# Block copies by DMA and 32x32 transposes on VectorE in place of TensorE transposes, in a two-layer cross-attention kernel

## What is computed

```
q = x Wq + bq;  k = ctx Wk + bk;  v = ctx Wv + bv
w = softmax(q k^T / sqrt(512)) over the 224 rows of x (axis 1), not over the 750 of the context
x = layernorm(w v + x) * gamma + beta
```

## Time and profile before

| what | value |
|---|---|
| three runs | 1115.15, 1117.38 (median), 1117.8 us |
| profiled execution | span 1115.5 us from its first to its last instruction; what lies around the span is not listed |
| span against the median | 1.9 us shorter |
| busy share of the span: PE, PEld, DVE, ACT, POOL | 94, 88, 79, 71, 70% |
| DMA queues | 60 MB, 16.8% of 16 engines |

### The profile page before, as it was taken

How to read it: one execution, slowest core, us unless ns; L and a number is a source line. 1 busy time by engine, 2 the same in 40 slices (tenths; PEclk the granted TensorE clock), 3 DMA queues, 4 the chain that set the end, 5 groups by cost and what they waited for, 6 DMA issues and landing times.

```text
span 1115.5 us, 26568 instructions
## 1 busy us (share of the span) xinstructions
PE 1050.1 (94%) x8392; PEld 981.2 (88%) x8392; DVE 879.5 (79%) x2561; ACT 788.8 (71%) x2033; POOL 775.8 (70%) x646
## 2 busy tenths in 40 slices
PE   4999999999999999999999999999999999999973
PEld 3888999899989999999999989998998999899973
DVE  1557888888888888888888888888888888888864
ACT  1446777777777777777777777777777777777733
POOL 0034787777777877777787777777877777778754
PEclk8898999999999999999999999999999999999987
DMA  8121101111110111111101111111011111111001
GB/s 214 40 87 40 37 32 62 62 62 60 60 44 33 44 60 60 60 60 56 41 26 58 60 60 60 60 51 39 31 60 60 60 60 60 44 35 43 18 17 33
DMA packets 19218, 60.15 MB, mean 54 GB/s; under 512 B 4064, under 2 KB 6112, under 8 KB 19184
## 3 DMA queue, kind: packets, MB, share of 16 engines
q1 hardware_dynamic: 16544, 59.71, 16.4%
q10 hardware_dynamic: 2640, 0.01, 0.2%
HBM read 45.03 MB, written 14.68 MB: 54 GB/s over the span
## 4 chain that ended last, share of the span: by engine, by line
PE 84%; DVE 6%; issue 5%; ACT 3%; DMA 2%; POOL 0%; SPq 0%; DVEq 0%; POOLq 0%; ACTq 0%
PE score_bank L551 8%; PE oq_bank L568 8%; PE oq_bank L570 8%; PE oq_bank L569 8%; PE score_bank L553 7%; PE score_bank L552 7%; PE oq_bank L526 5%; PE oq_bank L524 5%; PE oq_bank L525 5%; PE pv_bank L599 4%; PE pv_bank L597 4%; PE pv_bank L598 4%; PE t_bank L474 3%; PE t_bank L492 3%; PE oq_bank L575 2%
## 5 line engine op out<-in xcount | busy, mean ns | idle before, releaser
L751 ACT ACTIVATE probs<-scores,neg_max 125x224 f32<-125x224 f32 x384 | 180.8, 474 | 128.7 <-DVE neg_max L955 128.6
L568 PE MATMUL oq_bank<-pr_hi,cn_hi 125*128 125x224 f32 x768 | 214.0, 279 | 13.8 <-DVE pr_lo L970 9.9
L551 PE MATMUL score_bank<-qT_hi,cT_hi 128*125 128x224 f32 x768 | 218.2, 284 | 6.2 <-DVE qT_lo L939 6.2
L570 PE MATMUL oq_bank<-pr_hi,cn_lo 125*128 125x224 f32 x768 | 212.9, 277 | 0.0
L569 PE MATMUL oq_bank<-pr_lo,cn_hi 125*128 125x224 f32 x768 | 212.6, 277 | 0.0
L553 PE MATMUL score_bank<-qT_hi,cT_lo 128*125 128x224 f32 x768 | 209.0, 272 | 0.0
L552 PE MATMUL score_bank<-qT_lo,cT_hi 128*125 128x224 f32 x768 | 208.7, 272 | 0.0
L1154 POOL TENSOR_TENSOR cn_lo<-raw,cn_hi 125x768 fp32r<-125x768 f32 x64 | 139.7, 2183 | 99.1 <-ACT cn_hi L708 97.9
L1176 POOL TENSOR_TENSOR rstd<-ve,minus_half 112x1 f32<-112x1 f32 x128 | 85.1, 665 | 135.4 <-DVE ve L1025 135.2
L955 DVE CUSTOM_DVE_ANT_0 scores<-score_bank,d_row 125x224 f32<-125x224 f32 x384 | 138.8, 380 | 32.0 <-PE score_bank L553 28.8
L568 PEld LDWEIGHTS oq_bank<-pr_hi,cn_hi 125*128 125x128 f32 x768 | 149.6, 195 | 15.2 <-issue 10.7
(11 more groups left out here) (105 smaller groups left out, 2945.1 us busy)
## 6 DMA issues: line engine op xcount, KB each, us to landing
raw<-in_ctx_dram SPq DMA_DIRECT2D x32, 750.0 KB
x<-in_x_dram SPq DMA_DIRECT2D x32, 448.0 KB, 4.9
out_dram<-y_out SPq DMA_DIRECT2D x31, 448.0 KB, 3.3
y<-in_L_xattn_Wq_dram SPq DMA_DIRECT2D x4, 512.0 KB, 10.5
x<-in_L_xattn_Wk_dram SPq DMA_DIRECT2D x2, 512.0 KB, 9.9
x<-in_L_xattn_Wv_dram SPq DMA_DIRECT2D x2, 512.0 KB, 11.3
bv_row<-in_L_xattn_bv_dram SPq DMA_DIRECT2D x2, 256.0 KB, 7.0
gamma_row<-in_L_xattn_gamma_dram SPq DMA_DIRECT2D x2, 256.0 KB, 7.8
```

The costliest lines, as they stand in the source:

```text
L551: nc.tensor.matmul(o, hi, qT_hi[:, l, :], start=(l == 0), stop=False)
L568: nc.tensor.matmul(o, hi, pr_hi[0:MP, u.par, c, :], start=(c == 0), stop=False)
L570: ins = nc.tensor.matmul(o, lo, pr_hi[0:MP, u.par, c, :], start=False, stop=(c == MC - 1))
L751: ins = act.activation(probs[0:MP, u.par, c, :], scores[0:MP, c, :], ACT.Exp, bias=neg_max[0:MP, c:c + 1], scale=-1.0, accum_out=ssum[0:MP ...
```

## The change

Both transposes on TensorE of layer 0 go. SyncE loads each x and each context a second time, in blocks: the piece of 32 rows x 32 columns that one VectorE transpose turns lies on 32 partitions, in runs of 32 numbers (128 B). Per batch these are 16 DMAs for x and 12 for the context. VectorE turns them (`turn_x` twice 128 x 448, `turn_ctx` four times 128 x 384) into one SBUF buffer of two halves, `turned`, from which ScalarE makes the high parts, VectorE the low part of x (line 908 before, now from SBUF) and GpSimd the low part of the context (line 900 before, four pieces in place of three). Layer 1's x is still transposed by TensorE. `raw` has one buffer in place of two; rows of x go as "(h p)" and of the context as "(c p)", so a partition's row is no longer one run.

In every product the matmuls with high moving parts come first and those with low ones last. `score_max` writes into `probs`. `add_eps`, `inverse_deviation` and `shift` take both halves at once. The slots become turns of two units (a is 2i, b is 2i+1, counted from there), with a new order on each engine (ScalarE's is not shown); some steps lie further behind than before, such as `add_pv(b(-2), 1)`.

```diff
-        raw = sb("raw", [P, 2, MC, L])
+        raw = sb("raw", [P, MC, L])
+        xb = sb("xb", [P, EC, XC, RB])
+        cb = sb("cb", [P, LC, CC, RB])
+        turned = sb("turned", [P, 2, 2 * T])
...
+        def turned_x(g):
+
+            return turned[:, g, :].rearrange("p (e t) -> p e t", e=2)
+
+        def turned_ctx(g):
+
+            return turned[:, g % 2, 0:LC * PC].rearrange("p (l m) -> p l m", l=LC)
+
+        def piece(g):
+
+            return slice(g * PC, min((g + 1) * PC, M))
...
+            def load_xb(u):
+                if not u.real:
+                    return
+                if u.past(-2):
+
+                    sp.wait_ge(x_turned, u.batch(2))
+                    sp.sem_inc(wait_alone, 1)
+                blocks = x[u.batch()].rearrange("(c r) (k b s) -> b k r c s", r=RB, k=EC, s=RB)
+                for b in range(P // RB):
+                    for k in range(EC):
+                        sp.dma_start(xb[b * RB:(b + 1) * RB, k, :, :], blocks[b, k]).then_inc(xb_loaded, 16)
+
+            def load_cb(u):
+                if not u.real:
+                    return
+                if u.past(-2):
+
+                    sp.wait_ge(ctx_turned, u.batch(PIECES))
+                    sp.sem_inc(wait_alone, 1)
+                src = ctx[u.batch()]
+                full = src[0:CFULL * RB, :].rearrange("(c r) (k b s) -> b k r c s", r=RB, k=LC, s=RB)
+                rest = src[CFULL * RB:M, :].rearrange("r (k b s) -> b r k s", k=LC, s=RB)
+                for b in range(P // RB):
+                    for k in range(LC):
+                        sp.dma_start(cb[b * RB:(b + 1) * RB, k, 0:CFULL, :], full[b, k]).then_inc(cb_loaded, 16)
+                    sp.dma_start(cb[b * RB:b * RB + CREST, :, CFULL, :], rest[b]).then_inc(cb_loaded, 16)
...
+            start = Unit(0)
             load_qk(0)
-            load_x(0)
-            load_ctx(0)
+            load_xb(start)
+            sp.wait_ge(cb_cleared, 1)
+            load_cb(start)
+            load_x(start)
+            load_ctx(start)
...
+            def turn(i, j):
+                a, b = units(i, j)
+                if a(+1).later(1):
+                    load_xb(a(+1))
+                store(b(-3))
+                if a(+1).later(1):
+                    load_x(a(+1))
+                if a(+0).later(0):
+                    load_ctx(a(+0))
+                if a(+1).later(1):
+                    load_cb(a(+1))
+            turns(sp, turn)
...
+                o = oq_bank[l][:, 0:T]
                 for e in range(EC):
                     if l == 0 and e % 2 == 0:
                         pe.wait_ge(xT_hi_done, u.n(m=2, add=e // 2 - 1))
+                    nc.tensor.matmul(o, A_hi[:, u.layer, e, l * P:(l + 1) * P], xT_hi[:, e, :], start=(e == 0), stop=False)
+                    nc.tensor.matmul(o, A_lo[:, u.layer, e, l * P:(l + 1) * P], xT_hi[:, e, :], start=False, stop=False)
+                for e in range(EC):
+                    if l == 0 and e % 2 == 0:
                         pe.wait_ge(xT_lo_done, u.n(m=2, add=e // 2 - 1))
-                    hi = A_hi[:, u.layer, e, l * P:(l + 1) * P]
-                    lo = A_lo[:, u.layer, e, l * P:(l + 1) * P]
-                    o = oq_bank[l][:, 0:T]
-                    nc.tensor.matmul(o, hi, xT_hi[:, e, :], start=(e == 0), stop=False)
-                    nc.tensor.matmul(o, hi, xT_lo[:, e, :], start=False, stop=False)
-                    ins = nc.tensor.matmul(o, lo, xT_hi[:, e, :], start=False, stop=(e == EC - 1))
+                    ins = nc.tensor.matmul(o, A_hi[:, u.layer, e, l * P:(l + 1) * P], xT_lo[:, e, :],
+                                           start=False, stop=(e == EC - 1))
                 ins.then_inc(q_ready, 1)
...
+            def turn(i, j):
+                a, b = units(i, j)
+                q_product(b(-1), 0)
+                spread_d(b(-1))
+                q_product(b(-1), 1)
+                pv_product(b(-2), 1)
+                score_product(b(-1), 0)
+                score_product(b(-1), 1)
+                score_product(b(-1), 2)
+                o_product(a(-1), 0)
+                o_product(a(-1), 1)
+                if j is None and i == 0:
+                    transpose_weights(0)
+                    fold_weights(0)
+                    fold_c(0)
+                    fold_w(0)
+                q_product(a(+0), 0)
+                pv_product(a(-1), 0)
+                spread_d(a(+0))
+                pv_product(a(-1), 1)
+                q_product(a(+0), 1)
+                if j is None and i == 0:
+                    transpose_weights(1)
+                o_product(b(-1), 0)
+                score_product(a(+0), 0)
+                score_product(a(+0), 1)
+                o_product(b(-1), 1)
+                transpose_x(b(+0), 0)
+                transpose_x(b(+0), 1)
+                score_product(a(+0), 2)
+                if j is None and i == 0:
+                    fold_beta()
+                    fold_weights(1)
+                    fold_c(1)
+                    fold_w(1)
+                pv_product(b(-1), 0)
+            turns(pe, turn)
...
+            def turn_x(u, g):
+                if not u.real:
+                    return
+                if g == 0:
+                    dve.wait_ge(xb_loaded, u.batch(XB_DMAS * 16, XB_DMAS * 16))
+                if u.past(-2):
+
+                    dve.wait_ge(ctxT_lo_done, u.batch(PIECES, g - 1))
+                dve.transpose(turned[:, g, :], xb[:, 2 * g:2 * g + 2, :, :].rearrange("p k c s -> p (k c s)")).then_inc(x_turned, 1)
+
+            def turn_ctx(u, g):
+                if not u.real:
+                    return
+                if g == 0:
+                    dve.wait_ge(cb_loaded, u.batch(CB_DMAS * 16, CB_DMAS * 16))
+                if g < 2:
+
+                    dve.wait_ge(xT_lo_done, u.n(m=2, add=g - 1))
+                else:
+                    dve.wait_ge(ctxT_lo_done, u.batch(PIECES, g - 1))
+                src = cb[:, :, :, :].rearrange("p l c s -> p l (c s)")[:, :, g * PC:(g + 1) * PC]
+                dve.transpose(turned_ctx(g), src).then_inc(ctx_turned, 1)
...
-                dve.tensor_tensor_reduce(scores[0:MP, c, :], b[0:MP, (c % 2) * T:(c % 2 + 1) * T], d_row[0:MP, :], -SCALE,
-                                         3.4e38, ALU.add, ALU.min, neg_max[0:MP, c:c + 1]).then_inc(smax_done, 1)
+                dve.tensor_tensor_reduce(probs[0:MP, u.par, c, :], b[0:MP, (c % 2) * T:(c % 2 + 1) * T], d_row[0:MP, :], -SCALE,
+                                         3.4e38, ALU.add, ALU.min, neg_max[0:MP, u.par, c:c + 1]).then_inc(smax_done, 1)
...
+            def add_eps(u):
+                if not u.real:
+                    return
+                dve.wait_ge(mv_done, u.n(m=2))
+                dve.tensor_scalar(ve[0:TP, u.par, :], mv[0:TP, u.par, :, 1], EPS, None, ALU.add).then_inc(ve_done, 1)
+
+            def shift(u):
+
+                if not u.real:
+                    return
+                dve.wait_ge(rstd_done, u.n())
+                dve.scalar_tensor_tensor(out=nmr[0:TP, u.par, :], in0=mv[0:TP, u.par, :, 0], scalar=-1.0,
+                                         in1=rstd[0:TP, u.par, :], op0=ALU.mult, op1=ALU.mult).then_inc(nmr_done, 1)
...
+            def turn(i, j):
+                a, b = units(i, j)
+                xT_lo_part(a(+0), 1)
+                add_pv(b(-2), 1)
+                turn_ctx(a(+0), 1)
+                invert_sum(b(-1), 0)
+                half_moments(b(-2), 1)
+                score_max(b(-1), 4)
+                o_lo(a(-1), 0)
+                moments(b(-2), 1)
+                score_max(b(-1), 5)
+                add_eps(b(-2))
+                dot(a(+0), 1)
+                turn_ctx(a(+0), 2)
+                shift(b(-2))
+                o_lo(a(-1), 1)
+                residual(a(-1), 0)
+                invert_sum(b(-1), 1)
+                residual(a(-1), 1)
+                q_lo(a(+0), 0)
+                turn_ctx(a(+0), 3)
+                add_pv(a(-1), 0)
+                probs_lo(b(-1), 0)
+                probs_lo(b(-1), 1)
+                add_pv(a(-1), 1)
+                q_lo(a(+0), 1)
+                if j is None and i == 0:
+                    WqT_out(1)
+                half_moments(a(-1), 0)
+                half_moments(a(-1), 1)
+                moments(a(-1), 0)
+                moments(a(-1), 1)
+                add_eps(a(-1))
+                o_lo(b(-1), 0)
+                score_max(a(+0), 0)
+                score_max(a(+0), 1)
+                shift(a(-1))
+                if j is None and i == -1:
+                    WqT_out(0)
+                    A_lo_part(0)
+                    take_c(0)
+                    take_w(0)
+                turn_x(a(+1), 0)
+                score_max(a(+0), 2)
+                turn_x(a(+1), 1)
+                score_max(a(+0), 3)
+                dot(b(+0), 0)
+                dot(b(+0), 1)
+                invert_sum(a(+0), 0)
+                o_lo(b(-1), 1)
```

(62 more changed lines are left out.)

570 lines of the change are left out of this document (189 added, 381 removed).

## The result

| | median | runs | from to |
|---|---|---|---|
| before | 1117.6 us | 4 | 1115.2 to 1120.6 |
| after | 1249.6 us | 4 | 1247.2 to 1250.9 |

The ratio is 1.118, interval 1.116 to 1.120: the changed kernel is slower by 132 us, where 46 us less was forecast. It lies above the stated range too, which ended at 1151.

What follows compares the result with a forecast made beforehand. TensorE was taken to bound the kernel before, and the shared port the changed one at 30.8 us a batch: 1115.5 - 42 (loop) - 4 (start) = 1069.5, with 1.9 for median above span 1071 us; range 1025 to 1151.

Steps and rivals of the forecast that it cites:

- What bounds the kernel before: Loop before the change: TensorE sets the pace, busy 31.3 of 32.1 us a batch; the port did not bind.
- TensorE: TensorE in the loop: without the transposes, 2.1 us a batch, its own pace becomes 29.5 us.
- B: Rival for the loop: the port does not bind, TensorE still does at 28.9 to 29.9 a batch, 1027 us; chance 0.22.
- VectorE's own work: VectorE in the loop: 2.0 and 0.6 us leave, six transposes add 3.2; busy time from 26.8 to about 27.4.
- GpSimd: GpSimd in the loop: four low parts of the context add 4.0 us, its unblocked work becomes 25.4 a batch.
- The shared port: SBUF port pair of VectorE and GpSimd: its line takes 30.8 us a batch and sets the pace, 42 us saved.
- 14 x 0.47: Shared port: 14 VectorE users a batch each add a mean 0.47 us to GpSimd's line of 25.4, making 32.0.
- 0.40 to 0.58 us are added: Shared port: the time each blocking adds to an instruction, read from the trace as agreeing with an exclusive lock.
- Rival C: Rival for the loop: VectorE becomes the bound by port waits of 6.7 us, 33.3 a batch, 1151 us; chance 0.20.
- DMA: Transfers in the loop: 599 pieces of 128 B per engine at 19 ns, 11.4 us; 17 of 31 us, hidden.
- D: Rival for the transfers: the 128 B pieces bind, at 60 ns each 42 us a batch, 1430 us; chance 0.07.
- Start and end: Outside the loop: TensorE's 9.4 us wait for the context goes, 28 issues delay weights; 4 us saved, end as before.

Runs made afterwards that it cites:

- b_out_vector: The kernel before, with layer 1's scale and add_beta on VectorE in place of GpSimd: 1127.4 us, ratio 1.011.
- b_port_load: The kernel before, with four more GpSimd subtractions a batch on a spare SBUF tile that nothing waits for: 1177.8 us, ratio 1.055.
- a_narrow_short: The changed kernel with GpSimd's scale and add_beta over 64 columns and VectorE's turns over 32: 1093.6 us, ratio 0.981.
- b_both: The kernel before in its old engine orders, with six VectorE transposes and four GpSimd subtractions a batch more on spare tiles: 1235.2 us, ratio 1.108.
- The long runs: The changed kernel with the blocks of x and the context filled by one transfer each, in long contiguous runs: 1241.2 us, ratio 1.111.
- the short turns: The changed kernel with each of VectorE's six turns of a batch over 32 columns only: 1235.1 us, ratio 1.105.

## Why the prediction was wrong

- **What bounds the kernel before**: right, TensorE. b_out_vector takes 2.1 of the port's 31.1 us away and gains nothing. But it was no bound by itself: 3.3 us of spare GpSimd work cost 2.1 (b_port_load).
- **TensorE**: own pace 29.5 was too low. The transposes' 2.1 measure 31.3 - 30.2 = 1.1 in busy time, and the lowest batch seen is 31.2, in a_narrow_short. So even B, in which the port does not bind, would have given about 1094, not 1027.
- **VectorE's own work**: right. Turns 0.57 and 0.63 (0.5 and 0.6 forecast), 3.5 us in all (3.2); own work 26.5 (26.6).
- **GpSimd**: `ctxT_lo` alone takes 0.94 (1.0 forecast), but GpSimd idles 6.6 us a batch, where hardly any was forecast.
- **The shared port**: here it failed. The rule was right and was priced from the rows; the sum was put on the wrong engine. "14 x 0.47" went onto GpSimd's line, and VectorE's own waits were left at what the old kernel shows, 0.1 per user; they measure 0.54 per user, 8.7 us a batch. "0.40 to 0.58 us are added" already leaves out the residual's 0.91, which stands a few sentences ahead of it. A wait on GpSimd is short, some 0.45, since VectorE's instructions are short; a wait on VectorE is the rest of an instruction of 1.3 to 2 us, at times one more. The step "in-order engines cannot use such a line wholly ... I take 30.8 itself" dropped the one term that mattered.
- **Rival C** is what came: VectorE without idle time, means of residual, `pr_lo` and `dot` over 1 us. Its size was off: waits 6.7 forecast and 8.7 measured (16 users with `shift`, 0.54 each, where it priced 14 at 0.48), and 1.0 of idle time that it left out; 26.5 + 8.7 + 1.0 = 36.2 against 33.3. Of the 1.0 idle, 0.6 goes with the lower granted clock, which the prediction has nowhere. What was held against C, the small waits of the old kernel, was no guide: the same two kinds of work raise them there from 1.3 to 4.4, and the batch to 36.0 (b_both). So added work alone can bring about such a batch, though there by another mix, 4.4 of waits and 4.1 of idle time; in the new orders the waits are twice that. The slack of GpSimd and of VectorE was largely one and the same, and both were filled.
- **DMA**: hidden, as forecast; D is excluded. The piece of 128 B was priced at 19 ns between bounds of 13.5 and 177 and measures 13.0; the DMA share is 0.37, where near 0.5 was forecast.
- **Start and end**: 4 us saved was forecast, 2 to 3 came. The long runs show that the small issues cost 8 us there.

Open: how the lower clock and the longer batches hang together; why the short turns give 0.5 of 2.3 us is told only as far as VectorE's idle time shows; which other engine's result it then waits for in each place was not isolated. A version with the new transposes in the old orders, and nothing else new, was not built.

## What to carry to other kernels

Idle time of GpSimd is not free for more GpSimd work while VectorE's instructions with two SBUF inputs fit into it: add up both engines' use of the port, then put the waits on the engine with the shorter instructions, since it waits for the longer ones. Before moving work off the engine that paces, ask what the next one has left after its waits have grown, not after its work has. And try the parts of a change singly: here the order of the matmuls paid 0.8% by itself. When a mean period moves, look at single batches and their granted clock before giving the whole difference to the edit.
